# Numerators and denominators of the attend pass as fp32 products in four column tiles

## What is computed

```python
B, S, D = x.shape                      # 8, 1024, 512
H, K, M = 16, 32, 128                  # heads, width of a head, features
pq = _phi(q * scale, omega)            # [B, S, H, M] features of the queries
pk = _phi(k * scale, omega)            # features of the keys
kv = einsum('bhsm,bhsk->bhmk', pk, v)  # [B, H, M, K] sums over a batch
z = sum(pk, axis=2)                    # [B, H, M]
num = einsum('bhsm,bhmk->bhsk', pq, kv)
den = einsum('bhsm,bhm->bhs', pq, z)
out = num / den[..., None]             # then @ wo, residual, layer norm, feed-forward
```

## Time and profile before

| | |
|---|---|
| timed runs | 3478.57, 3481.13, 3484.28 us; median 3481.13 us |
| span of the profiled execution | 3482.2 us, first to last instruction; no time outside it is listed |
| attend pass | about 917 to 2070 us |
| PE busy | 3422.0 us, 98% |
| DVE, ACT, POOL busy | 71%, 57%, 32% |

### The profile page before, as it was taken

One profiled execution on the slowest core, in us unless ns is written; L12 is line 12 of the kernel. 1 busy time (PEld: TensorE's weight loads), 2 busy tenths in 40 slices (PEclk: granted clock), 3 DMA queues, 4 the chain that ended last, 5 costly groups with the idle time before them and its releaser, 6 DMA issues.

```text
span 3482.2 us, 77456 instructions
## 1 busy us (share of the span) xinstructions
PE 3422.0 (98%) x29993; PEld 3151.9 (91%) x29993; DVE 2468.2 (71%) x4839; ACT 1969.8 (57%) x4240; POOL 1105.2 (32%) x861
## 2 busy tenths in 40 slices
PE   8999999999899999999999999999999999999998
PEld 6888888888788888888888889999999999999998
DVE  6767777677667777677777766666666666666666
ACT  6777777777556666666656654444444444444443
POOL 3554554545345454555555532000000000000000
PEclk9999999999899999999999999999999999999999
DMA  3222222222323333232332346444444444444443
GB/s 128 80 77 74 95 77 83 77 74 77 107 79 114 106 102 115 82 126 94 102 109 93 111 144 206 147 148 148 147 146 146 146 146 146 146 146 146 146 147 126
DMA packets 195355, 409.83 MB, mean 118 GB/s; under 512 B 27440, under 2 KB 52528, under 8 KB 194992
## 3 DMA queue, kind: packets, MB, share of 16 engines
q1 hardware_dynamic: 194992, 404.89, 34.6%
HBM read 292.50 MB, written 112.33 MB: 116 GB/s over the span
## 4 chain that ended last, share of the span: by engine, by line
PE 70%; DVE 2%; ACT 1%; issue 0%; POOL 0%; DMA 0%; ACTq 0%; POOLq 0%; DVEq 0%
PE ffn_hidden L175 30%; PE attend_gated L175 20%; PE ffn_result L175 8%; PE attend_num L175 6%; PE attend_feat L1425 3%; PE attend_feat L1445 1%; PE ffn_turn L1910 1%; PE attend_turn L1415 1%; DVE attend_kvz_lo L1393 1%; DVE attend_pT_lo L1354 1%; PE attend_feat L1452 1%; PE attend_turn L1434 0%; ACT attend_kvz_hi L1300 0%; DVE attend_kvz_lo L1396 0%; DMA ffn_r_in<-in_L_attn_w_dram 0%
## 5 line engine op out<-in xcount | busy, mean ns | idle before, releaser
L175 PE MATMUL ffn_hidden<-ffn_yT_hi,ffn_wa_hi 128*128 128x256 f32 x2048 | 574.1, 280 | 3.5 <-DVE ffn_wa_lo L1798 1.8
L175 PE MATMUL ffn_hidden<-ffn_yT_lo,ffn_wa_hi 128*128 128x256 f32 x2048 | 573.3, 280 | 0.0
L175 PE MATMUL ffn_hidden<-ffn_yT_hi,ffn_wa_lo 128*128 128x256 f32 x2048 | 572.0, 279 | 0.0
L316 POOL TENSOR_TENSOR ffn_n_rstd<-ffn_n_base,ffn_n_power 128x2 f32<-128x2 f32 x32 | 27.5, 860 | 1300.1 <-DVE ffn_n_negmean L311 1300.1
L1780 ACT ACTIVATE ffn_ht_hi<-ffn_hs 128x512 fp32r<-128x512 f32 x248 | 156.4, 631 | 420.6 <-DVE ffn_hs L1827 420.6
L175 PEld LDWEIGHTS ffn_hidden<-ffn_yT_hi,ffn_wa_hi 128*128 128x128 f32 x2048 | 385.0, 188 | 4.4 <-DVE ffn_wa_lo L1798 2.3
L175 PEld LDWEIGHTS ffn_hidden<-ffn_yT_hi,ffn_wa_lo 128*128 128x128 f32 x2048 | 385.2, 188 | 0.0
L175 PEld LDWEIGHTS ffn_hidden<-ffn_yT_lo,ffn_wa_hi 128*128 128x128 f32 x2048 | 384.9, 188 | 0.2
L635 POOL TENSOR_TENSOR keys_z_sum<-keys_z_sum,keys_e 128x512 f32<-128x512 f32 x192 | 259.6, 1369 | 232.9 <-ACT keys_e L703 232.9
L1831 DVE TENSOR_TENSOR ffn_ht_lo<-ffn_hs,ffn_ht_hi 128x512 fp32r<-128x512 f32 x248 | 173.6, 700 | 218.9 <-ACT ffn_ht_hi L1780 218.9
L1765 ACT ACTIVATE ffn_hid<-ffn_hidden,ffn_bias 128x256 f32<-128x256 f32 x496 | 206.1, 467 | 180.5 <-PE ffn_hidden L175 180.5
(11 more groups left out here) (305 smaller groups left out, 11669.3 us busy)
## 6 DMA issues: line engine op xcount, KB each, us to landing
ffn_tq<-part_d SPq DMA_DIRECT2D x248, 512.0 KB, 3.9
keys_xin<-in_L_attn_x_dram SPq DMA_DIRECT2D x32, 512.0 KB, 4.5
xn_d<-keys_xn SPq DMA_DIRECT2D x32, 512.0 KB, 3.0
xT_d<-keys_xT_whole SPq DMA_DIRECT2D x32, 512.0 KB, 2.6
u_d<-keys_uq SPq DMA_DIRECT2D x32, 512.0 KB, 3.1
shared_xTf<-xT_d SPq DMA_DIRECT2D x32, 512.0 KB, 6.0
shared_uq<-u_d SPq DMA_DIRECT2D x32, 512.0 KB, 4.9
r_d<-shared_gate SPq DMA_DIRECT2D x32, 512.0 KB, 3.1
```

What stands on the lines that cost most here:

```text
L175: last = pe.matmul(out, stationary[a], moving[b], start=start and n == 0, stop=stop and n == len(TERMS) - 1)
```

## The change

The twelve split products of a num step become eight fp32 products. Each has 32 stationary columns (a head's kv, or its z in the first of 32 columns), all 128 rows and 256 moving columns. Head j writes to output partitions 32 j to 32 j + 31: numerators into the first half of the bank, denominators into the second. The features are exp + FLOOR in fp32, made by one DVE operation from the bank; ACT no longer rounds them, and pT.lo goes. The sums kvz are fp32, copied by two ACT instructions at the start of a batch; DVE's kv job goes. The tables lose DVE's "kv" and ACT's "hi"; the denominators are stored by one DMA instead of two, and DVE's "o" is one instruction on 128 partitions instead of two on 64.

```diff
-        pT = [Pair(mem, ctx, f"pT{j}", [P, 2 * GT]) for j in range(HC)]
-        kvz = Pair(mem, ctx, "kvz", [P, NC, HC, P])
+        pT = [sb(f"pT{j}_hi", [P, 2 * GT]) for j in range(HC)]
+        kvz = sb("kvz_hi", [P, NC, HC, 2 * KD])
...
-                    for pp in range(2):
-                        row = pair_of(2 * pp)[1]
-                        sp.dma_start(den_d[g][pp], raw[row:row + 2, :, pp * GT:(pp + 1) * GT]).then_inc(den_stored, 16)
+                    sp.dma_start(den_d[g], raw[0:P:KD, :, GT:2 * GT]).then_inc(den_stored, 16)
...
-            def round_up(cc, j, g):
-                act.wait_ge(e_ready[j], 2 * g + cc + 1)
-                wait(act, num.full, NC * g + 2 * cc)
-                act.activation(pT[j].hi[:, :], feat[j].t[:, :], ACT.Copy, bias=FLOOR).then_inc(pT_hi[j], 1)
...
-                    for j in range(HC):
-                        at, row = pair_of(j)
-                        act.activation(kvz.hi[:, :, j, row:row + 1], kv_in[:, :, j, KD:KD + 1], ACT.Copy, bias=FLOOR * S)\
-                            .then_inc(kvz_hi, 1)
-                        act.activation(kvz.hi[:, :, j, at:at + KD], kv_in[:, :, j, 0:KD], ACT.Copy).then_inc(kvz_hi, 1)
+                    act.activation(kvz[:, :, :, KD:KD + 1], kv_in[:, :, :, KD:KD + 1], ACT.Copy, bias=FLOOR * S)\
+                        .then_inc(kvz_ready, 1)
+                    act.activation(kvz[:, :, :, 0:KD], kv_in[:, :, :, 0:KD], ACT.Copy).then_inc(kvz_ready, 1)
...
-                        dve.wait_ge(pT_hi[j], 2 * g + n + 1)
-                        dve.scalar_tensor_tensor(out=pT[j].lo[:, :], in0=feat[j].t[:, :], scalar=FLOOR,
-                                                 in1=f32(pT[j].hi[:, :]), op0=ALU.add, op1=ALU.subtract)\
-                            .then_inc(feat[j].free, 1)
+                        dve.wait_ge(e_ready[j], 2 * g + n + 1)
+                        wait(dve, num.full, NC * g + 2 * n)
+                        dve.tensor_scalar(pT[j][:, :], feat[j].t[:, :], FLOOR, None, ALU.add).then_inc(feat[j].free, 1)
...
-                    for pp in range(2):
-                        dve.tensor_tensor(o[rows_of(pp), :, :], raw[rows_of(pp), :, pp * GT:(pp + 1) * GT],
-                                          o[rows_of(pp), :, :], ALU.mult).then_inc(o_ready, 1)
+                    dve.tensor_tensor(o[:, :, :], raw[:, :, 0:GT], o[:, :, :], ALU.mult).then_inc(o_ready, 1)
...
-                    for j in range(HC):
-                        last = product(pe, num.t[:, j // 2 * GT:(j // 2 + 1) * GT], kvz[:, n, j, :],
-                                       pT[j][:, n % 2 * GT:(n % 2 + 1) * GT], start=j % 2 == 0, stop=j % 2 == 1)
+                    for part in range(2):
+                        for j in range(HC):
+                            last = pe.matmul(num.t[rows(j), part * GT:(part + 1) * GT],
+                                             kvz[:, n, j, part * KD:(part + 1) * KD],
+                                             pT[j][:, n % 2 * GT:(n % 2 + 1) * GT], start=True, stop=True)
```

More of the change, by code:

```diff
@@ L1030, in attend_pass @@
         q_turned, q_split = early.q_turned, early.q_split
-        kvz_cleared, kvz_hi, kvz_ready = sem("kvz_cleared"), sem("kvz_hi"), sem("kvz_ready")
+        kvz_cleared, kvz_ready = sem("kvz_cleared"), sem("kvz_ready")
         squared, sq_ready = sem("squared"), sem("sq_ready")
@@ L1065, in attend_pass @@
                    ("num", 2, 0)]
-        DVE_BODY = [("top", 0, 0), ("top", 1, 0), ("recip", 0, -1), ("below", 0, 0), ("mix", 0, 1), ("kv", 0, 0),
-                    ("exp", 0, 0), ("o", 0, -1), ("out", 0, 0), ("sq", 0, 1), ("turn_q", 0, 1), ("sq", 1, 1),
+        DVE_BODY = [("top", 0, 0), ("top", 1, 0), ("recip", 0, -1), ("below", 0, 0), ("mix", 0, 1), ("exp", 0, 0), ("o", 0, -1), ("out", 0, 0), ("sq", 0, 1), ("turn_q", 0, 1), ("sq", 1, 1),
                     ("out", 1, 0), ("mix", 1, 1), ("hi", 1, 0), ("turn_q", 1, 1), ("wo", 0, -1), ("wo", 1, -1),
@@ L1242, in do @@
                 if job == "exp":
-                    exps(n, 0, g)
                     for j in range(HC):
[L1245 to L1248, removed]
-                if job == "hi":
-                    for j in range(HC):
-                        round_up(n, j, g)
+                        exps(n, j, g)
                 if job == "num":
                     act.wait_ge(num.full, NC * g + n + 1)
-                    wait(act, o_ready, 2 * g)
-                    wait(act, den_stored, 32 * g)
+                    wait(act, o_ready, g)
+                    wait(act, den_stored, 16 * g)
                     act.activation(raw[:, n, :], num.t[:, :], ACT.Copy).then_inc(num.free, 1)
                 if job == "oT":
-                    act.wait_ge(o_ready, 2 * g + 2)
+                    act.wait_ge(o_ready, g + 1)
                     for t in range(TG):
@@ L1388, in do @@
                             .then_inc(part_ready, 1)
-                if job == "kv":
-                    dve.wait_ge(kvz_hi, 2 * HC * b + 2 * HC)
-                    for j in range(HC):
-                        at, row = pair_of(j)
-                        dve.scalar_tensor_tensor(out=kvz.lo[:, :, j, row:row + 1], in0=kv_in[:, :, j, KD:KD + 1],
-                                                 scalar=FLOOR * S, in1=f32(kvz.hi[:, :, j, row:row + 1]),
-                                                 op0=ALU.add, op1=ALU.subtract)
-                        last_kv = dve.tensor_tensor(kvz.lo[:, :, j, at:at + KD], kv_in[:, :, j, 0:KD],
-                                                    f32(kvz.hi[:, :, j, at:at + KD]), ALU.subtract)
-                    last_kv.then_inc(kvz_ready, 1)
             run(dve, do, DVE_BODY)
@@ L1457, in do @@
                     if n == 0:
-                        pe.wait_ge(kvz_ready, b + 1)
+                        pe.wait_ge(kvz_ready, 2 * b + 2)
                     wait(pe, num.free, NC * g + n)
@@ L1716, in do @@
                     if n == NH - 1:
-                        act.wait_ge(left.o_ready, 2 * G)
+                        act.wait_ge(left.o_ready, G)
                     for k in (2 * n, 2 * n + 1):
```

32 lines of the change are left out of this document (11 added, 21 removed).

## The result

| | before | after |
|---|---|---|
| timed runs | 3478.57 to 3487.75, median 3482.70 us (4 runs) | 3422.87 to 3426.97, median 3426.32 us (4 runs) |
| profiled execution | span 3482.2 us | span 3423.9 us, own time 3426.44 us |
| ratio after / before | | 0.9839, 95% interval 0.9826 to 0.9853 |

The kernel became 56 us faster; 82 us slower was predicted (3563 against the 3481 us of before). The time is close to that of rival 1, which had been worked out to 3421 us and given 0.07.

The account below looks back on a forecast made before the run. PE, 98% of the span, was taken to bound the kernel: 3482.2 + 73.6 (num steps) + 17 (edges) - 8.3 (waits) = 3564.5 us, so a median of about 3563; range 3530 to 3770.

Parts of the forecast that it names:

- rival 1: Num steps: four column tiles run together, unhindered by program order; 0.89 us a step, about 3421 us; chance 0.07.
- How far the sixteen passes overlap: Num steps: a product waiting for its tile holds all behind it; 2.01 us a step against 1.43, +73.6 us.
- What bounds the kernel: Whole kernel: PE's products cover 98% of the 3482.2 us span; the attend pass is a stream of PE work.
- What is removed: Num steps on PE: twelve products of 256 moving columns, a body of 1.43 us a step, 5.73 us a group.
- What is added: Num steps on PE: eight fp32 products a step, sixteen passes of 256 columns, taken at 0.223 us each.
- the lower bound of 0.12: Num steps: least time in us for an fp32 pass, that of a one-pass product of 256 columns.
- 9 slots: Num steps: eight products run as a staircase, never more than two passes together; 9 x 0.223 = 2.01 us a step.
- Edges: Attend pass, PE switching between 128-row work and tiles: gaps of +0.53 us a group, +17 us, bounds 0 to 30.
- Waits that go: Second feat at batch starts: PE's wait for the kv work of ACT and DVE goes, 1.18 us x 7 batches, -8.3 us.
- Edits at nothing: Attend pass: ACT's 256 roundings, DVE's addition and o product, and one SP store lie under PE, worth nothing.
- rival 3: Num steps: column tiles don't overlap at all, sixteen passes in a row, 3.57 us a step, about 3763 us; chance 0.13.

Follow-up runs that it names:

- the first experiment: Changed kernel with the four passes of each head in an attend_num step written one behind the other on its tile: median 3426.09 us, ratio 0.9841 to before.
- the run with the narrow product: Changed kernel plus a product of 2 moving columns, 32 stationary columns on the first column tile, between numerators and denominators of every attend_num step: 3429.4 us.

## Why the prediction was wrong

**The step that failed is "How far the sixteen passes overlap"**, and in it the reading of the earlier trace rows. The prediction saw that head 0's third product started only at 1518.33, when head 3's second did, and took head 3 for the cause. Two readings fitted those rows: head 3 held the others back, or something else held all four heads. A place where no head is late tells them apart, and feat 0 of the same group is one. The timeline of PE of the kernel before:

```profile
1509.43 0.39 PE L1445 MATMUL attend_feat<-shared_qT_hi,shared_omegaT_hi 32*128 32x256 f32 x4
1509.65 0.29 PE L1445 MATMUL attend_feat<-shared_qT_hi,shared_omegaT_lo 32*128 32x256 f32 x4
```

All four heads start together here, and the second products still stand 0.22 us behind the first, as far as 1518.33 stands behind 1518.11. The same delay stands behind the edge of the earlier trace rows (1534.03 to 1534.26, 0.23 us), where the prediction itself had put it down to the edge. The weight loads at the place of the earlier trace rows, a view that the prediction didn't look at, show where the time goes:

```profile
1518.10 0.29 PEld L1445 LDWEIGHTS attend_feat<-shared_qT_hi,shared_omegaT_lo 32*128 32x128 f32 x4
1518.21 0.30 PEld L1445 LDWEIGHTS attend_feat<-shared_qT_lo,shared_omegaT_hi 32*128 32x128 f32 x4
```

The loads for the products that start at 1518.33 begin at 1518.21, 0.11 us behind the first of those ahead of them, and each product follows the start of its own load by 0.12 us. So head 0 wasn't ready at 1518.23, when the prediction wanted it to go on. By themselves the loads don't decide, since head 3's load for its second product begins at 1518.21 too (the row x4 ends at 1518.39, a load takes 0.18). But a few rows on the starts leave the program's order, if by only some thousandths of a microsecond:

```profile
1518.92 0.28 PE L1452 MATMUL attend_feat<-attend_belowT,attend_pick 32*128 32x256 f32 x2
1518.92 0.27 PE L1445 MATMUL attend_feat<-shared_qT_lo,shared_omegaT_hi 32*128 32x256 f32 x1
```

In the program the products of qT_lo with omegaT_hi of all four heads stand ahead of the first one with belowT; here two heads' last products start ahead of another head's third. The run with reordered row tiles confirms it on the chip. The rule of the Trainium skill that went with the reading (TensorE: Matmul & The Clock Gate, Part 3: Packing small matmuls: matmuls start and end strictly in the order of the program) doesn't hold between tiles in the two runs that put a tile's products one behind the other. The run with a tile's passes in a row contradicts it most plainly, with 1.02 us a step where that order of starts asks for 2.9. What the Trainium skill says in TensorEngine Tiling, Key Properties (tiles operate independently) is what was measured.

One thing in the earlier trace rows does hold what follows it in the program: a wait for another engine. Head 0's second product starts at 1518.11, 1.2 us after its first (1516.91) and right behind head 3's first, which waited for DVE. So a product that waits for its tile lets other tiles pass, and one that waits for another engine doesn't.

**Point by point:**

- What bounds the kernel: right. PE is 98% busy before and after, and the time follows its jobs.
- What is removed, 5.73 us a group of step body: right by the steps of the earlier trace rows.
- What is added, sixteen passes of 0.223 us: right in kind, 4% high (0.214). The fold of the earlier trace rows gave a good price, and the lower bound of 0.12 didn't come into it.
- Overlap: wrong, as said. 4 rounds instead of 9 slots are 5 x 0.223 us less in each of 128 steps, 143 us; that alone turns the prediction of 3563 into rival 1's 3421.
- Edges, +17 us: right in mechanism, somewhat small. A step pays 0.14 us inside, 0.56 in a group. Behind it "out" takes 3.00 us (2.80 before, 1520.77 to 1523.57 in the earlier trace rows), and turn_q (0.06), k and wo (0.09 each) are longer too, 0.44 together. The four steps of before exceeded their 5.73 by 0.29. So 0.56 + 0.44 - 0.29 = 0.71 us a group, 23 us in 32 groups, inside the stated 0 to 30. (The 30 isn't what its words give: five edges with an entry of 0.08 and an exit of 0.19 each are 1.35 us a group, 43 us.)
- Waits that go, -8.3 us: right in place and size. Put back, the job makes the attend pass 8.2 us longer in the traces (5.8 by the medians), and feat 1 at a batch's start is 1.18 us longer again, as the earlier trace rows had it.
- Edits at nothing: right. 138 us of ScalarE's roundings put back change nothing.

The sum with the two terms put right: 128 x (4 x 0.214 - 1.43) = -73.5, +23, -8.3, together -59 us. From the first num step to the job behind the last, the traces have 1121.70 us before (946.70 to 2068.40) and 1062.82 after, 58.9 less, and the span fell by 58.3.

The chances failed with the reading. One place, read from starts alone, was taken as enough to put the case that the row tiles' groups of four spoke for at 0.07. The whole range, 3530 to 3770, lay on the wrong side.

## What to carry to other kernels

Small products on different tiles of PE needed no interleaving by hand here: what counts is the longest tile's own chain of passes (here 4 x 0.21 us), and what each change of tiling costs (0.14 us where one was taken away, at most 0.19 where two were put in), so tiled jobs belong next to each other. A wait for another engine ahead of one tile's product does stop the others. Where a product starts late, look for a place where its neighbours are on time before blaming them: if it is as late there, it waits for something of its own, such as its weights.

## What the hardware showed that was not expected

- Products on different tiles start out of the program's order: with sixteen passes written tile by tile, the fourth tile's first pass starts within 0.08 us of the first tile's (rows of the first experiment), ahead of nine passes that precede it in the program.
- Four column tiles, each with all 128 rows, cost no more than one: 0.21 us a round on one, two or four. That they read the same 128 partitions at once, the ground of rival 3, costs nothing that these runs show.
- An fp32 pass of 256 columns takes 0.21 us, so a product (two instructions) 0.43 us, 3.6 of the 0.12 us of an fp32r product of the earlier trace rows.
- A product of 2 moving columns over the whole array, between tiled products, costs 0.41 us more than one on a single tile.
- A signal on the last product of a step need not come behind all tiles. In the run with the narrow product the first tile has two short passes more. The product that carries the step's signal is the fourth tile's and starts its last pass at 1472.48, and the first tile's last pass starts after it (the timeline of PE, in a view that holds this pass alone):

```profile
1472.50 0.38 PE L1426 MATMUL attend_num<-attend_pT_hi,attend_kvz_hi 128*32 128x256 f32 x1
```
